# First units of a gated cross-attention block in another order on all engines: ScalarE widens the first quantised inputs, the query halves are projected first, and group 1's weights are prepared after the first unit's heads

## The chip, the cores and the metric

One core of a Trainium2 chip (trn2) runs one program. Its engines are TensorE (PE in the profile, PEld its weight loads), VectorE (DVE), ScalarE (ACT), GpSimd (POOL) and SyncE (SP), which only issues DMAs here. Each runs its own list of instructions in the written order and waits on semaphores for the others. The metric is the device time in microseconds (us) of one execution, the median of several. For the kernel before that is 700.87 us (three runs, 699.86 to 701.37).

## What is computed

The part that matters is the attention on 4 batches of 256 rows of 256 values; a mixture of 8 experts (2 per row) follows it.

```python
ln_out = _ln(hidden_states, ln_w, ln_b)
q = _fp8_linear_pertensor(ln_out, wq, wq_scale, q_in_scale)      # per head: _ln(q, qln_w, qln_b); the same for k
v = _fp8_linear_pertensor(ln_out, wv, wv_scale, v_in_scale)
core = _gqa(q, k, v)                                             # softmax(q k / sqrt(d)) v, 16 query heads on 8 groups
qx = _ln(_fp8_linear_pertensor(ln_out, wqx, wqx_scale, qx_in_scale), qxln_w, qxln_b)
kx, vx = split(einsum(cond, w_kv_x)); kx = _ln(kx, kxln_w, kxln_b)
xout = _gqa(qx, kx, vx)
catq = _div_clamp_fp8(cat(core, xout), proj_smooth)
x = x + tanh(g_xattn[0]) * einsum(catq, wproj) * (proj_in_scale * proj_w_scale)
x = x + tanh(g_ffn[0]) * moe(_layernorm(x))
```

`_fp8_linear_pertensor` divides its input by a scale per column, clips it to 448, rounds it to bf16 and then to fp8, and multiplies by the weights.

## The kernel before, in words

**Units.** The attention is cut into 32 units: unit u = 4g + b is head group g (of 8) on batch b (of 4). A unit has two row tiles of 128 rows (st = 0, 1). For each unit TensorE projects queries (`project_q`, L335) and keys and values (`project_kv`, L347 and, for the other input, L351), turns the heads (`turn_heads`, L408), multiplies scores (`scores`, L379), turns probabilities (`turn_probs`, L394) and multiplies values (L419). ScalarE sums the squares of the heads (`square_q` L671, `square_kv` L679, with the copy of the values L684), GpSimd takes the inverse root (`power`, L1425 and L1427), VectorE multiplies by it (`normalise_q` L947, `normalise_kv` L956 to L963), ScalarE scales the turned heads (`affine`, L714), and GpSimd and VectorE split them into a high and a low part (`heads_hi` L1444 and `split_heads` L981, L985). Scores then go through `row_max` (L990, VectorE), `exps` (L698, ScalarE), the inverse of the sum (L995, VectorE) and `scale_probs` (L1433, GpSimd).

**Inputs.** The rows of x come in three chunks: chunks 0 and 1 are two row tiles each (batches 0 and 1), chunk 2 is the other four. A chunk is normalised by rows (VectorE for chunk 0, ScalarE's `row_scale`, L777, for the others; the inverse root is GpSimd's `row_power`, L1484 and L1486, and `row_shift`, L1492 and L1494), turned on TensorE (`turn_input`, L456), scaled by ScalarE (`affine_in`, L754), clipped and rounded by VectorE (`quantise_in`, L1098 and L1104) and widened to fp32r by GpSimd (`widen_in`, L1509) into the tile `xq`, part by part: parts 0 to 3 are chunk 0, parts 4 to 7 chunk 1, 8 to 15 chunk 2. The other input, ctx, is split by ScalarE (`split_ctx`, L761) and VectorE (`ctx_rest`, L1118).

**Weights.** A group's weights are loaded raw into the tile `spare` (in the code `w_raw`), summed (`sum_weights`, L1050, L1053), centred and scaled in blocks of 128 columns (`centre_weights`, L1061, L1063, on VectorE; half of group 0's, `centre_first`, L1502, on GpSimd), and split in four parts into a high part (`weights_hi`, L743, ScalarE) and a low part (`weights_lo`, L1071, VectorE) in `w_ring`. SyncE loads group g's raw weights when the low parts of group g - 1 are done (`w_ready`).

**What sets the order.** Nothing is scheduled by a program: each engine's list is written by hand, for the start line by line and for units 1 to 28 in a loop (`steps`, L238). The change touches only what stands ahead of that loop.

## Time and profile before

| | us |
|---|---|
| median of three runs | 700.87 (699.86 to 701.37) |
| span of the profiled execution | 698.4 |
| what lies around it (median less span) | 2.5 |
| TensorE busy | 640.8 (92%) |
| VectorE busy | 600.3 (86%) |
| ScalarE busy | 550.0 (79%) |
| GpSimd busy | 464.4 (67%) |

The profile is of one execution on the core. "Busy" leaves out waits on semaphores. Times in a timeline are from the start of the span, and a row that stands for several instructions ("x4") gives in its second column the time from the start of the first to the end of the last. In brackets stands how long the engine had been idle before the row and which instruction of which engine ended that. PEclk is TensorE's granted clock as a share of full speed (2.4 GHz).

### The profile page before, as it was taken

How to read it: one execution, taken by the hardware profiler on the slowest of the kernel's cores; microseconds unless marked ns; L12 is line 12 of the kernel's file. 1: busy time of each engine (PE TensorE's matmuls, PEld its weight loads, DVE VectorE, ACT ScalarE, POOL GpSimd, SP SyncE). 2: the span in 40 equal slices, each digit the busy share in tenths (PEclk: the TensorE clock that was granted, in tenths of full speed). 3: DMA queues.
4: the chain of work that ended last, by engine and by line, in shares of the span. 5: the costliest groups of instructions: out<-in, count | busy, mean ns of one | idle time of the engine just before them, and what ended most of it. 6: DMA issues, size and time to landing. Idle time of an engine off the chain costs nothing. (4 is left out here: it accounts for less than half of the span.)

```text
span 698.4 us, 14919 instructions
## 1 busy us (share of the span) xinstructions
PE 640.8 (92%) x4548; PEld 586.4 (84%) x4549; DVE 600.3 (86%) x1387; ACT 550.0 (79%) x1927; POOL 464.4 (67%) x646
## 2 busy tenths in 40 slices
PE   1579999999999999999999999999998569999994
PEld 0578899999999999999999999999977457888883
DVE  7787899999989999998999999888898777777772
ACT  5787889988998999899899989988874145566671
POOL 4777777688677768867776886787664425554542
PEclk9969999999999999999999999999999569999998
DMA  7101101021020101102000110100098402333232
GB/s 224 61 1 52 41 1 31 2 61 32 1 61 2 31 1 62 31 1 61 1 32 1 54 44 1 61 1 1 1 376 317 159 30 47 53 53 52 46 42 26
DMA packets 35509, 37.72 MB, mean 54 GB/s; under 512 B 2704, under 2 KB 30352, under 8 KB 35440
## 3 DMA queue, kind: packets, MB, share of 16 engines
q1 hardware_dynamic: 31024, 30.84, 13.3%
q0 software_dynamic: 4416, 6.03, 5.4%
q8 instruction: 34, 0.56, 0.3%
q14 instruction: 35, 0.29, 0.1%
...
## 5 line engine op out<-in xcount | busy, mean ns | idle before, releaser
L1433 POOL TENSOR_SCALAR shared<-shared,rsum 128x256 f32<-128x256 f32 x256 | 143.5, 572 | 55.6 <-DVE rsum L995 50.6
L698 ACT ACTIVATE shared<-s,nmax 128x256 f32<-128x256 f32 x256 | 122.2, 498 | 23.2 <-DVE nmax L990 23.1
L1427 POOL TENSOR_TENSOR rstd<-rstd,half 128x7 f32<-128x7 f32 (+1 forms) x64 | 87.9, 1374 | 5.3
L990 DVE TENSOR_REDUCE nmax<-s 128x2 f32<-128x512 f32 x128 | 86.5, 678 | 2.8 <-PE s L379 2.6
L1000 DVE TENSOR_TENSOR pt_lo<-t,pt_hi 128x512 fp32r<-128x512 f32 x124 | 84.1, 678 | 1.9 <-ACT pt_hi L706 0.9
L706 ACT CAST pt_hi<-t 128x512 fp32r<-128x512 f32 x124 | 74.0, 597 | 9.8 <-PE t L394 7.3
L714 ACT ACTIVATE shared<-route_bank,head_w 128x512 f32<-128x512 f32 (+1 forms) x124 | 81.5, 689 | 0.0
L394 PE MATMUL t<-ident,shared 128*128 128x128 f32 x496 | 75.8, 276 | 5.8 <-POOL shared L1433 2.5
L985 DVE TENSOR_TENSOR qk_lo<-shared,qk_hi 128x512 fp32r<-128x512 f32 x96 | 78.2, 814 | 2.5 <-POOL qk_hi L1444 1.4
L335 PE MATMUL pj_a<-w_ring,xq 128*128 128x256 f32 x488 | 72.7, 292 | 6.8 <-POOL xq L1509 6.8
L1984 DVE TENSOR_TENSOR w_lo<-expert_w,w_hi 128x1024 fp32r<-128x1024 f32 x46 | 56.3, 1225 | 25.8 <-ACT w_hi L1861 25.1
L379 PE MATMUL s<-qk_hi 128*128 128x256 f32 x256 | 77.9, 304 | 0.2 <-DVE qk_lo L985 0.2
L379 PE MATMUL s<-qk_hi,qk_lo 128*128 128x256 f32 x256 | 72.7, 284 | 0.0
L379 PE MATMUL s<-qk_lo,qk_hi 128*128 128x256 f32 x256 | 72.6, 284 | 0.0
L335 PEld LDWEIGHTS pj_a<-w_ring,xq 128*128 128x128 f32 x488 | 63.5, 193 | 7.3 <-POOL xq L1509 7.2
L438 PE MATMUL acc_bank<-wp_ring,cq 128*128 128x256 f32 x496 | 69.4, 283 | 0.0
L394 PEld LDWEIGHTS t<-ident,shared 128*128 128x128 f32 x496 | 57.7, 141 | 13.7 <-issue 3.7
L729 ACT ACTIVATE y_bf<-o_bank,inv_smooth 128x256 bf16<-128x256 f32 x128 | 54.2, 482 | 18.5 <-PE o_bank L419 18.0
L1451 POOL TENSOR_SCALAR cq<-y_bf 128x512 fp32r<-128x512 f16 x64 | 39.7, 620 | 42.2 <-DVE y_bf L1010 42.1
L438 PEld LDWEIGHTS acc_bank<-wp_ring,cq 128*128 128x128 f32 x496 | 65.4, 190 | 2.5
L671 ACT ACTIVATE start<-pj_a 128x128 bf16<-128x128 f32 x244 | 64.6, 290 | 2.9 <-PE pj_a L335 2.9
L947 DVE TENSOR_TENSOR start<-pj_a,rstd 128x512 f32<-128x512 f32 x61 | 41.9, 687 | 21.6 <-POOL rstd L1427 21.1
...
## 6 DMA issues: line engine op xcount, KB each, us to landing
...
```

Source lines behind the costliest of these rows:

```text
L335: m = pe.matmul(to[:, c0:c0 + 2 * D], xq[:, typ, k, t0:t0 + P], w_ring[:, par, part, k, c0:c0 + 2 * D], start=i == 0, stop=i == 3)
L379: m = pe.matmul(s_bank[st][:, h * S:(h + 1) * S], l[:, qc:qc + P], r[:, kc:kc + S], start=i == 0, stop=i == 2)
L394: m = pe.transpose(to[:, c:c + P], probs[:, st, h * S + kt * P:h * S + (kt + 1) * P], ident[:])
L438: m = pe.matmul(to, cq[:, b % 2, a, h * S + st * P:h * S + (st + 1) * P], wp_ring[:, par, part, 2 * a + h, :], start=n == 0, stop=n == 7)
L698: e = act.activation(probs[:, st, h * S:(h + 1) * S], s_bank[st][:, h * S:(h + 1) * S], ACT.Exp, bias=nmax[:, st, h:h + 1], accum_out=psum ...
L706: act.copy(pt_hi[:, :, st * P:(st + 1) * P], turned(u, a, st)[:].rearrange("p (n s) -> p n s", n=4)).then_inc(pthi_done, 1)
L714: m = act.activation(qk[:, at + c0:at + c0 + n], src[:, c0:c0 + n], ACT.Identity, scale=head_w[:, 2 * w:2 * w + 1], bias=head_w[:, 2 * w + ...
L985: dve.tensor_tensor(qk_lo[:, to], qk[:, c], qk_hi[:, to].bitcast(F32), ALU.subtract).then_inc((qsplit_done, ksplit_done, xsplit_done)[i], 1)
L990: dve.tensor_reduce(nmax[:, st, :], s_bank[st][:].rearrange("p (h t) -> p h t", h=2), AX, ALU.max, negate=True).then_inc(max_done, 1)
L1000: dve.tensor_tensor(pt_lo[:, :, c], turned(u, a, st)[:].rearrange("p (n s) -> p n s", n=4), pt_hi[:, :, c].bitcast(F32), ALU.subtract).the ...
L1427: pool.tensor_tensor(rstd[:, st, c], rstd[:, st, c], half[:, c], ALU.pow).then_inc(rstd_ready, 1)
L1433: m = pool.tensor_scalar(probs[:, st, c], probs[:, st, c], rsum[:, st, h:h + 1], 1.0, ALU.mult, ALU.mult)
```

## The change

Four things change in the written lists ahead of unit 1. ScalarE widens parts 0 to 3 (`widen_first`), and GpSimd keeps parts 4 to 15; chunk 1's rows are normalised by GpSimd and no longer by ScalarE. TensorE projects the queries of both row tiles of the first unit ahead of its keys and values, and group 0's weight parts are made in the order 2, 0, 3, 1 (`FIRST_PARTS`). Further on, unit 0's first `power`, `normalise_q` and `normalise_kv` come earlier in the lists of GpSimd and VectorE. Group 1's raw weights are summed and centred by VectorE, and split by ScalarE, behind the first unit's heads. Semaphores follow: `own_q_centred`, `first_q_ready` and `first_widened` are new. SyncE's list of DMAs is the same.

```diff
--- before.py
+++ after.py
...
+        FIRST_PARTS = (2, 0, 3, 1)
...
@@ -459,19 +462,22 @@
             pe.wait_ge(cols_loaded, 32)
             turn_input(0)
             turn_input(1)
-            pe.wait_ge(xq_ready, 4)
-            pe.wait_ge(w_ready, 1)
+            pe.wait_ge(first_widened, 2)
+            pe.wait_ge(first_q_ready, 1)
             for n in range(2):
                 project_q(0, 0, 0, n, early_banks[n][0], 0)
-                if n == 0:
-                    pe.wait_ge(ctx_split, 1)
+            pe.wait_ge(first_widened, 3)
+            pe.wait_ge(w_ready, 1)
+            pe.wait_ge(ctx_split, 1)
+            for n in range(2):
                 project_kv(0, 0, 0, n, early_banks[n][1], 0)
-            pe.wait_ge(xq_ready, 8)
+            pe.wait_ge(xq_ready, 2)
+            project_q(1, 0, 1, 0, o_bank, 0)
+            pe.wait_ge(xq_ready, 4)
             pe.wait_ge(ctx_split, 2)
-            project_q(1, 0, 1, 0, o_bank, 0)
             project_kv(1, 0, 1, 0, acc_bank, 0)
+            turn_heads(0, 0, 0, s_bank[0])
             turn_input(2)
-            turn_heads(0, 0, 0, s_bank[0])
             turn_heads(0, 0, 1, s_bank[1])
             turn_heads(0, 0, 2, pj_b)
             project_q(1, 0, 1, 1, pj_a, 1)
...
@@ -750,7 +757,7 @@
                 c, col_i, src, to = input_tile(n)
                 act.wait_ge(zt_done, c + 1)
                 if n >= 20:
-                    act.wait_ge(xq_ready, n - 11)
+                    act.wait_ge(xq_ready, n - 15)
                 act.activation(to, src, ACT.Identity, scale=in_scale[:, col_i:col_i + 1],
                                bias=in_shift[:, col_i:col_i + 1]).then_inc(xq_y, 1)
 
@@ -770,9 +777,15 @@
                 square_q(v, st, early_banks[n][0])
                 square_kv(v, v, st, early_banks[n][1])
 
+            def widen_first(m):
+
+                _, _, y, to = input_part(m)
+                act.wait_ge(xq_grid, m + 1)
+                act.activation(to, y.rearrange("p (k t) -> p k t", k=to.shape[1]), ACT.Copy, scale=1.0 / GRID).then_inc(first_widened, 1)
+
             def row_scale(c):
 
-                act.wait_ge(ln_shift, c)
+                act.wait_ge(ln_shift, 1)
                 for t in range(*chunks[c]):
                     m = act.activation(acc[:, t, :], acc[:, t, :], ACT.Identity, scale=lnr[:, t:t + 1], bias=ln_mr[:, t:t + 1])
                 m.then_inc(z_ready, 1)
@@ -780,24 +793,33 @@
             act.wait_ge(consts_ready, 1)
             for n in range(8):
                 affine_in(n)
-            row_scale(1)
             weights_hi(0, 0, 2)
+            weights_hi(0, 0, 0)
+            for n in range(8, 10):
+                affine_in(n)
+            widen_first(0)
+            widen_first(1)
             weights_hi(0, 0, 3)
-            weights_hi(0, 0, 0)
+            for n in range(10, 12):
+                affine_in(n)
             weights_hi(0, 0, 1)
             split_ctx(0)
-            for n in range(8, 16):
+            widen_first(2)
+            square_q(0, 0, early_banks[0][0])
+            for n in range(12, 14):
                 affine_in(n)
+            square_q(0, 1, early_banks[1][0], other_junk[0])
+            square_kv(0, 0, 0, early_banks[0][1])
+            for n in range(14, 16):
+                affine_in(n)
+            square_kv(0, 0, 1, early_banks[1][1], other_junk[1])
+            widen_first(3)
             split_ctx(1)
-            square(0)
+            row_scale(2)
             act.wait_ge(v0_scaled, 1)
             act.copy(v0_w[:, 0], v0_raw).then_inc(v0_high, 1)
-            square(1)
-            row_scale(2)
+            square(2)
             split_ctx(2)
-            square(2)
-            weights_hi(1, 1, 0)
-            weights_hi(1, 1, 1)
             affine(0, 0, s_bank[0])
             act.wait_ge(v0_ready, 1)
             affine(0, 1, s_bank[1])
@@ -806,6 +828,8 @@
             for n in range(16, 20):
                 affine_in(n)
 
+            weights_hi(1, 1, 0)
+            weights_hi(1, 1, 1)
             weights_hi(1, 1, 2)
             weights_hi(1, 1, 3)
             exps(0, 0, 0)
...
@@ -1063,15 +1087,19 @@
                         m = dve.tensor_scalar(w, w, w_scale[:, k, at:at + 1], None, ALU.mult)
                 if n == later_blocks(g)[-1]:
                     m.then_inc(w_centred, 1)
+                elif g == 0 and n == 3:
+                    m.then_inc(own_q_centred, 1)
 
             def weights_lo(g, par, c):
-                dve.wait_ge(w_hi_done, 4 * g + ((c + 2) % 4 if g == 0 else c) + 1)
+                dve.wait_ge(w_hi_done, 4 * g + (FIRST_PARTS.index(c) if g == 0 else c) + 1)
                 k, c0 = c // 2, (c % 2) * BLK // 2
                 c1 = min(c0 + BLK // 2, width(g))
                 m = dve.tensor_tensor(w_ring[:, par, 1, k, c0:c1], w_raw[:, k, c0:c1],
                                       w_ring[:, par, 0, k, c0:c1].bitcast(F32), ALU.subtract)
                 if c == (1 if g == 0 else 3):
                     m.then_inc(w_ready, 1)
+                elif g == 0 and c == 0:
+                    m.then_inc(first_q_ready, 1)
 
             def row_stats(c):
 
@@ -1148,33 +1176,35 @@
             sum_weights(0, 1)
             sum_weights(0, 0)
             dve.wait_ge(w_scales_ready, 1)
-            centre_weights(0, 0, (0, 1, 2, 3) + later_blocks(0))
-            quantise_in(0, 4)
+            centre_weights(0, 0, (0, 1, 2, 3))
+            quantise_in(0, 2)
             weights_lo(0, 0, 2)
+            weights_lo(0, 0, 0)
+            centre_weights(0, 0, later_blocks(0))
+            quantise_in(2, 4)
             weights_lo(0, 0, 3)
-            weights_lo(0, 0, 0)
             weights_lo(0, 0, 1)
             ctx_rest(0)
+            quantise_in(4, 6)
             row_stats(2)
-            quantise_in(4, 8)
-            ctx_rest(1)
             dve.wait_ge(v0_loaded, 16)
             dve.tensor_tensor(v0_raw, v0_raw, w_scale[:, :, 7:8].broadcast_to([P, KT, D]), ALU.mult).then_inc(v0_scaled, 1)
+            normalise_q(0, 0, 0, early_banks[0][0])
+            normalise_kv(0, 0, 0, early_banks[0][1])
+            quantise_in(6, 8)
+            ctx_rest(1)
+            normalise_q(0, 0, 1, early_banks[1][0])
+            normalise_kv(0, 0, 1, early_banks[1][1])
             dve.wait_ge(v0_high, 1)
             dve.tensor_tensor(v0_w[:, 1], v0_raw, v0_w[:, 0].bitcast(F32), ALU.subtract).then_inc(v0_ready, 1)
+            ctx_rest(2)
+            split_heads(0, 0, 0)
+            split_heads(0, 0, 1)
             for k in range(KT):
                 sum_weights(1, k)
             centre_weights(1, 0, (0, 1, 2, 3) + later_blocks(1))
-            normalise_q(0, 0, 0, early_banks[0][0])
-            normalise_kv(0, 0, 0, early_banks[0][1])
-            centre_weights(1, 1, (0, 1, 2, 3))
-            normalise_q(0, 0, 1, early_banks[1][0])
-            normalise_kv(0, 0, 1, early_banks[1][1])
-            ctx_rest(2)
-            split_heads(0, 0, 0)
-            split_heads(0, 0, 1)
-            centre_weights(1, 1, later_blocks(1))
             split_heads(0, 0, 2)
+            centre_weights(1, 1, (0, 1, 2, 3) + later_blocks(1))
             quantise_in(8, 10)
 
             row_max(0, 0, 0)
...
@@ -1485,12 +1515,19 @@
                 pool.wait_ge(var_eps0, c + 1)
                 pool.tensor_tensor(lnr[:, t], lnr[:, t], half[:, t], ALU.pow).then_inc(ln_rstd, 1)
 
+            def row_normalise(c):
+
+                pool.wait_ge(ln_rstd, c + 1)
+                for t in range(*chunks[c]):
+                    m = pool.tensor_scalar(acc[:, t, :], acc[:, t, :], mv[:, t, 0:1], lnr[:, t:t + 1], ALU.subtract, ALU.mult)
+                m.then_inc(z_ready, 1)
+
             def row_shift(c):
 
                 t = slice(*chunks[c])
                 pool.wait_ge(ln_rstd, c + 1)
                 pool.tensor_tensor(ln_mr[:, t], mv[:, t, 0], lnr[:, t], ALU.mult).then_inc(ln_shift_part, 1)
-                pool.wait_ge(ln_shift_part, c)
+                pool.wait_ge(ln_shift_part, 1)
                 pool.tensor_scalar(ln_mr[:, t], ln_mr[:, t], -1.0, 1.0, ALU.mult, ALU.mult).then_inc(ln_shift, 1)
 
             def centre_first():
@@ -1500,7 +1537,8 @@
                 for n in range(CENTRED[0]):
                     w, at = w_raw[:, 1, n * D:(n + 1) * D], SCALES[0][n]
                     m = pool.tensor_scalar(w, w, w_mean[:, 1, n:n + 1], w_scale[:, 1, at:at + 1], ALU.add, ALU.mult)
-                m.then_inc(first_centred, 1)
+                    if n in (3, CENTRED[0] - 1):
+                        m.then_inc(first_centred, 1)
 
             def widen_in(m):
 
@@ -1512,21 +1550,20 @@
             pool.wait_ge(ones_set, 1)
             row_power(0)
             row_power(1)
-            row_shift(1)
+            row_normalise(1)
             centre_first()
-            for m in range(4):
+            for m in range(4, 6):
                 widen_in(m)
             row_power(2)
             row_shift(2)
-            for m in range(4, 8):
+            power(0, 0)
+            for m in range(6, 8):
                 widen_in(m)
-            power(0, 0)
-            pool.wait_ge(normkv_done, 1)
             power(0, 1)
             wp_hi(0, 0, 0)
             wp_hi(0, 0, 1)
             heads_hi(0, 0, 0)
-            pool.wait_ge(normkv_done, 2)
+            pool.wait_ge(normkv_done, 1)
             power(1, 0)
             heads_hi(0, 0, 2)
             for m in range(8, 12):
@@ -1536,7 +1573,7 @@
             for m in range(12, 16):
                 widen_in(m)
             scale_probs(0, 0, 1)
-            pool.wait_ge(normkv_done, 3)
+            pool.wait_ge(normkv_done, 2)
             power(1, 1)
             scale_probs(0, 1, 0)
             wp_lo(0, 0, 0)
```

TensorE, start of the program, before: after the input is turned, the eight query matmuls of row tile 0 (into `pj_a`), its keys and values (`pj_b`), then row tile 1 (`s_0`).

```order
L335 MATMUL pj_a<-w_ring,xq 128x256 x8
L347 MATMUL pj_b<-w_ring,xq 128x256 x4
L351 MATMUL pj_b<-w_ring,ctx_hi 128x256 x2
L351 MATMUL pj_b<-w_ring,ctx_lo 128x256
L351 MATMUL pj_b<-w_ring,ctx_hi 128x256 x2
L351 MATMUL pj_b<-w_ring,ctx_lo 128x256
L335 MATMUL s_0<-w_ring,xq 128x256 x8
```

After:

```order
L338 MATMUL pj_a<-w_ring,xq 128x256 x8
L338 MATMUL s_0<-w_ring,xq 128x256 x8
L350 MATMUL pj_b<-w_ring,xq 128x256 x4
L354 MATMUL pj_b<-w_ring,ctx_hi 128x256 x2
L354 MATMUL pj_b<-w_ring,ctx_lo 128x256
L354 MATMUL pj_b<-w_ring,ctx_hi 128x256 x2
L354 MATMUL pj_b<-w_ring,ctx_lo 128x256
L350 MATMUL s_1<-w_ring,xq 128x256 x4
```

The eight query matmuls of row tile 1 now stand ahead of row tile 0's keys and values.

VectorE, from the low part of v0's weights (`cq`) to the second unit tile's normalise, before (`w_sum`, `w_mean` and `spare` with L1050 to L1063 are group 1's weights, `start<-pj_a,rstd` is the first normalise and `start<-s_0,rstd` the second):

```order
L1164 TENSOR_TENSOR cq<-shared,cq 128x256
L1050 TENSOR_REDUCE w_sum<-spare 128x5
L1053 TENSOR_SCALAR w_mean<-w_sum 128x5
L1050 TENSOR_REDUCE w_sum<-spare 128x5
L1053 TENSOR_SCALAR w_mean<-w_sum 128x5
L1061 TENSOR_SCALAR spare<-spare,w_mean,w_scale 128x128 x5
L1063 TENSOR_SCALAR spare<-spare,w_scale 128x128 x2
L947 TENSOR_TENSOR start<-pj_a,rstd 128x512
L956 TENSOR_SCALAR k_next<-pj_b,rstd 128x128
L957 TENSOR_TENSOR start<-pj_b,rstd 128x256
L963 TENSOR_TENSOR v_lo<-pj_b,v_hi 128x128
L1061 TENSOR_SCALAR spare<-spare,w_mean,w_scale 128x128 x4
```

After, from the scaling of v0's weights (`shared`) on (`start<-start` with L1126 and L1132 is the quantising of parts 6 and 7, `ctx_lo` the low part of ctx chunk 1):

```order
L1191 TENSOR_TENSOR shared<-shared,w_scale 128x256
L971 TENSOR_TENSOR start<-pj_a,rstd 128x512
L980 TENSOR_SCALAR k_next<-pj_b,rstd 128x128
L981 TENSOR_TENSOR start<-pj_b,rstd 128x256
L987 TENSOR_TENSOR v_lo<-pj_b,v_hi 128x128
L1126 TENSOR_SCALAR start<-start 128x512 x2
L1132 TENSOR_SCALAR start<-start 128x512 x2
L1146 TENSOR_TENSOR ctx_lo<-shared,ctx_hi 128x2x256
L971 TENSOR_TENSOR start<-s_0,rstd 128x512
```

Group 1's sums and first blocks no longer stand between v0's weights and the first normalise; quantising of parts 6 and 7 and a low part of ctx now stand between the first and the second normalise.

VectorE, the heads of unit 0 up to the quantising ahead of the first row max, before:

```order
L985 TENSOR_TENSOR qk_lo<-shared,qk_hi 128x512
L981 CAST qk_hi<-shared 128x512
L985 TENSOR_TENSOR qk_lo<-shared,qk_hi 128x512
L1061 TENSOR_SCALAR spare<-spare,w_mean,w_scale 128x128
L1063 TENSOR_SCALAR spare<-spare,w_scale 128x128 x2
L985 TENSOR_TENSOR qk_lo<-shared,qk_hi 128x512
```

After:

```order
L1009 TENSOR_TENSOR qk_lo<-shared,qk_hi 128x512
L1005 CAST qk_hi<-shared 128x512
L1009 TENSOR_TENSOR qk_lo<-shared,qk_hi 128x512
L1074 TENSOR_REDUCE w_sum<-spare 128x5
L1077 TENSOR_SCALAR w_mean<-w_sum 128x5
L1074 TENSOR_REDUCE w_sum<-spare 128x5
L1077 TENSOR_SCALAR w_mean<-w_sum 128x5
L1085 TENSOR_SCALAR spare<-spare,w_mean,w_scale 128x128 x5
L1087 TENSOR_SCALAR spare<-spare,w_scale 128x128 x2
L1009 TENSOR_TENSOR qk_lo<-shared,qk_hi 128x512
L1085 TENSOR_SCALAR spare<-spare,w_mean,w_scale 128x128 x5
L1087 TENSOR_SCALAR spare<-spare,w_scale 128x128 x2
```

The sums of group 1 and its ten centred blocks with their four plain scalings now stand between the second and the third `qk_lo` and behind the third, where one block and two plain scalings stood.

## Rows read from the trace of the kernel before

**Rows 1.** The page: the span, and from its part 5 GpSimd's scaling of probabilities

```profile
span 698.4 us, 14919 instructions
...
L1433 POOL TENSOR_SCALAR shared<-shared,rsum 128x256 f32<-128x256 f32 x256 | 143.5, 572 | 55.6 <-DVE rsum L995 50.6
```

**Rows 2.** Windows: length, busy us of each engine, PEclk, DMA share, GB/s

```profile
0.00:41.70 41.70, 18.41 (x114) 16.78 (x115) 31.39 (x115) 29.45 (x91) 24.63 (x40) 0.96 0.38 119
41.70:66.00 24.30, 19.00 (x123) 17.71 (x121) 19.37 (x48) 18.73 (x77) 18.85 (x25) 0.79 0.00 1
66.00:540.00 474.00, 467.91 (x3535) 439.68 (x3535) 439.94 (x1011) 420.54 (x1637) 351.10 (x524) 1.00 0.15 50
```

**Rows 3.** Waits from 66 to 540 us: the only one that a DMA ended

```profile
DVE w_sum L1050 <- DMA spare<-in_wT: 0.2, 1, 0.2
```

**Rows 4.** Waits from 30 to 66 us: in total, times, longest

```profile
DVE start L947 <- POOL rstd L1427: 5.7, 3, 3.8
```

**Rows 5.** Timeline of TensorE: start, us, line, tiles, forms, count, idle before

```profile
21.31 2.08 PE L335 MATMUL pj_a<-w_ring,xq 128*128 128x256 f32 x8 [6.83 <-POOL xq L1509]
23.18 1.05 PE L347 MATMUL pj_b<-w_ring,xq 128*128 128x256 f32 x4
```

**Rows 6.** Timeline of ScalarE, the start of the program

```profile
8.58 3.75 ACT L754 ACTIVATE start<-t,in_shift,in_scale 128x256 bf16<-128x256 f32 x8 [2.98 <-PE t L456]
...
13.69 2.18 ACT L743 CAST w_ring<-spare 128x512 fp32r<-128x512 f32 x4 [0.39 <-POOL spare L1502]
...
27.39 0.33 ACT L679 ACTIVATE start<-s 128x128 bf16<-128x128 f32 x1
...
28.28 2.15 ACT L777 ACTIVATE acc<-acc,ln_mr,lnr 128x256 f32<-128x256 f32 x4
30.26 1.11 ACT L761 CAST ctx_hi<-shared 128x1024 fp32r<-128x1024 f32 x1
...
35.54 0.78 ACT L714 ACTIVATE shared<-s,head_w 128x512 f32<-128x512 f32 x1 [1.17 <-PE s L408]
```

**Rows 7.** Timeline of GpSimd, the start of the program

```profile
10.59 3.07 POOL L1502 TENSOR_SCALAR spare<-spare,w_mean,w_scale 128x128 f32<-128x128 f32 x7 [0.78 <-DVE w_mean L1053]
14.94 6.31 POOL L1509 TENSOR_SCALAR xq<-start 128x512 fp32r<-128x512 f16 x4 [1.28 <-DVE start L1104]
...
23.57 2.36 POOL L1509 TENSOR_SCALAR xq<-start 128x512 fp32r<-128x512 f16 x4
...
26.58 1.73 POOL L1427 TENSOR_TENSOR rstd<-rstd,half 128x7 f32<-128x7 f32 x1
```

**Rows 8.** Timeline of VectorE, up to the first projections

```profile
11.79 2.46 DVE L1061 TENSOR_SCALAR spare<-spare,w_mean,w_scale 128x128 f32<-128x128 f32 x7
...
15.79 2.48 DVE L1071 TENSOR_TENSOR w_ring<-spare,w_ring 128x512 fp32r<-128x512 f32 x4
...
18.80 1.39 DVE L1081 BATCH_NORM_STATS2 stat<-acc 128x6 f32<-128x256 f32 x4
```

**Rows 9.** Timeline of VectorE, from v0's low part to the first row max

```profile
26.54 0.42 DVE L1164 TENSOR_TENSOR cq<-shared,cq 128x256 fp32r<-128x256 f32 x1 [3.00 <-ACT cq L794]
26.88 0.81 DVE L1050 TENSOR_REDUCE w_sum<-spare 128x5 f32<-128x640 f32 x1
...
28.74 1.36 DVE L1061 TENSOR_SCALAR spare<-spare,w_mean,w_scale 128x128 f32<-128x128 f32 x5
...
30.41 0.68 DVE L947 TENSOR_TENSOR start<-pj_a,rstd 128x512 f32<-128x512 f32 x1
...
31.80 1.10 DVE L1061 TENSOR_SCALAR spare<-spare,w_mean,w_scale 128x128 f32<-128x128 f32 x4
33.80 0.69 DVE L947 TENSOR_TENSOR start<-s,rstd 128x512 f32<-128x512 f32 x1 [0.90 <-POOL rstd L1427]
...
37.05 0.69 DVE L985 TENSOR_TENSOR qk_lo<-shared,qk_hi 128x512 fp32r<-128x512 f32 x1 [0.65 <-POOL qk_hi L1444]
...
38.12 0.69 DVE L985 TENSOR_TENSOR qk_lo<-shared,qk_hi 128x512 fp32r<-128x512 f32 x1
...
41.66 1.28 DVE L990 TENSOR_REDUCE nmax<-s 128x2 f32<-128x512 f32 x2
```

23 lines of the change are left out of this document (13 added, 10 removed).

## The prediction, made before the changed kernel ran

> **What bounds the kernel now.** I first read the windows [rows 2]. From 66 to 540 us TensorE is busy for 467.9 of 474.0 us at the full clock, and only one wait there was ended by a DMA, for 0.2 us [rows 3]. So that stretch neither absorbs nor adds anything: whatever the start of the program gains or loses is passed on. Up to 66 us it is different. TensorE is busy for 18.4 of the first 41.7 us and for 19.0 of the next 24.3, VectorE for 31.4 and 19.4. The end of that start is therefore set by a chain across the engines, which is read from the timelines.
>
> The reader is to see two things in them. At the front, TensorE stands idle for 6.83 us before its first projection at 21.31, released by GpSimd's widening [rows 5]; four widenings took 6.31 us there against 2.36 us for the next four, while VectorE worked through its low parts without a break [rows 7, 8]. That is the stall that the change goes at. Behind it, VectorE waits for 3.00 us before 26.54, then does group 1's sums and centring, and only then the first normalise at 30.41, although GpSimd's inverse root is done at 28.3 (26.58 + 1.73) [rows 7, 9]. After another 0.90 us of waiting the second normalise comes at 33.80, the second `qk_lo` at 38.12, and the first row max at 41.66 [rows 9]. I take the first row max as the milestone: from it on, VectorE and GpSimd pass the unit to each other.
>
> **Step A, the first projection.** VectorE now centres only four blocks first: 11.79 + 4 x 0.35 (2.46 / 7) = 13.2. Four parts were quantised between 14.2 and 15.8, so two cost 0.8: 14.0. Two low parts at 0.62 (2.48 / 4): 15.2 [rows 8]. On ScalarE the first high part waits for GpSimd's fourth block, 10.59 + 4 x 0.44 = 12.4 [rows 7]; two high parts at 0.54 and two input scalings at 0.47 give 14.4 [rows 6]. No row of before shows a widening on ScalarE. It writes 512 columns, so it lies between the cast of 512 columns (0.54) and the scaling of 512 columns (0.78) [rows 6]; I take 0.54 since it reads no table of scales: 15.5. With 0.5 for handovers the first projection starts at 16.0 in place of 21.31, 5.3 earlier. The higher price makes it 16.5, which nothing below depends on. Normalising chunk 1's rows on GpSimd is not shown either: between nothing beyond the two small operations that it replaces and 1.8 us (four blocks at 0.44 for two rows of 256 columns), which at worst moves GpSimd's centring by half a us; the same slack covers it.
>
> **Step B, the first and the second normalise.** TensorE needs 1.87 us for eight query matmuls (21.31 to 23.18) [rows 5], so 3.7 for both halves, about 2.2 for ten key and value matmuls, and ScalarE 0.9 for the squares (27.39 to 28.28) [rows 6]: the squares of row tile 0 are there at about 22.9. But GpSimd's list has the row statistics of chunk 2 ahead of `power(0, 0)`, and these wait for VectorE: from 15.2, three blocks 1.05, quantising 0.8, two low parts 1.2, a low part of ctx 0.6 (18.2 to 18.8 in before), quantising 0.8, and the row statistics 1.4 and an aggregation of about 0.3 give 21.4 [rows 8]. GpSimd's four small operations took 2.3 us (from 21.25, the end of its first widenings, to 23.57), so 23.7, and `power` 2.0 (the 1.73 and the small one ahead of it): 25.7 [rows 7]. First normalise at 25.8 in place of 30.41, 4.6 earlier. It takes 1.4 (30.41 to 31.80) [rows 9], then quantising 0.8 and ctx 0.6 follow: 28.6. GpSimd's widenings of parts 6 and 7 now stand behind `power(0, 0)`. They are ready at 28.0, and by the stretch of 6.31 us I hold them until VectorE pauses at 28.6; 2 x 0.59 gives 29.8, and `power(0, 1)` 1.9 more [rows 7]. Second normalise at 31.8 in place of 33.80: the lead has shrunk to 2.0.
>
> The Trainium skill has a rule on this, in the page "SBUF — State Buffer", section "SBUF: two separate sides": the port pair that VectorE and GpSimd share is an exclusive lock, and whoever starts first has it for one whole instruction. By that rule a widening would wait for one VectorE instruction, some 0.6 us, and the second normalise would come at most 0.6 earlier than I have it; the first widenings of this trace lost 4 us in one go [rows 7], so the trace agrees with a lock but not with a handover after each instruction. The sum goes by the row.
>
> **Step C, the heads.** TensorE's keys and values of unit 1 wait for that widening, 29.8. TensorE has little to do from about 24 on, so I price its ten matmuls at the half-speed pace of [rows 5], 2.2 us; at full speed they would be 1.1 less. ScalarE: squares 0.9 and the high part of ctx 1.0, so the first scaled heads start at 34.0 in place of 35.54 [rows 6]. The low part of ctx (1024 columns, twice 0.6) keeps VectorE until 35.2, and GpSimd's high part of the heads (about 0.6) follows: the first `qk_lo` at 35.9 in place of 37.05. From there to the end of the second `qk_lo` before took 1.7 us [rows 9], so 37.6 in place of 38.7. The lead is 1.1.
>
> **Step D, what is put in.** Here VectorE now does group 1's sums (26.88 to 28.74, 1.86), five blocks and two plain scalings (28.74 to 30.41, 1.67), the third `qk_lo` 0.6, and the same 1.67 once more: 5.8 us, and then the quantising, 0.8 [rows 9]. First row max at 37.6 + 5.8 + 0.8 = 44.2 in place of 41.66, **2.5 later**. Before, this work lay in the waits of 3.00 and 0.90 us and ahead of the first normalise; those waits are now longer and empty, and the work lies on the path. It costs 5.2 us in all (1.86 + 2 x 1.67), of which before only one block and two plain scalings, 0.8, stood behind the second `qk_lo`. ScalarE's high parts of group 1, moved behind the scaled inputs, stand ahead of `exps`, but are done while ScalarE would wait for the row max.
>
> **Step E, on to 66 us.** VectorE's waits for GpSimd's inverse root sum to 5.7 us there, the longest 3.8 [rows 4], and VectorE is idle for 4.9 us of 24.3 [rows 2]. Since GpSimd in turn waits for VectorE's row sums, as it does all along (55.6 us in the whole span, 50.6 of them so ended) [rows 1], a late VectorE delays the release of its own waits. I take 0.3 as given back, with 0 and 1.5 as the ends. The sum is 2.5 - 0.3 = +2.2 on a span of 698.4: 700.6. The median of the runs before, 700.87, stands 2.5 above that span, and I carry that: **703.1 us**.
>
> **The rivals.**
> *The front lead holds.* If the second normalise keeps the whole lead of 4.6 (29.2), the second `qk_lo` ends at 34.1, and the row max comes at 40.7, 1.0 earlier than before. With TensorE less often at half speed between 41.7 and 66 (granted 0.79 there [rows 2]) another 0.8 may go: 698.4 - 1.8 + 2.5 = 699.1. For it: the stall of 6.83 is the largest wait of the start. Against: GpSimd's widenings 6 and 7 and `power` alone take 3.1 us behind the first normalise's quantising. It decides where the second normalise comes before about 29.5 (31.8 less the 2.5 of step D), since the row max would then come as before.
> *The delay is absorbed.* If VectorE's waits give back 1.6 of their 5.7 us, +0.9: 701.8. For it, the 4.9 us idle; against it, the circular wait of step E.
> *It is worse.* GpSimd's widenings run beside VectorE's centring and quantising at the pace of the first four (1.6 each in place of 0.6), two ahead of the second normalise and two ahead of the first probabilities: + 2 to + 3, 705.6. It decides where VectorE has no pause between 26 and 29. This and the sum above lie on the slower side.
> *The order does nothing*, because ScalarE, with the added widenings, starts the first projection no earlier and the group 1 work falls into other waits: 700.9.
>
> **How the numbers follow.** Chances: the sum 0.56, lead holds 0.13, absorbed 0.14, worse 0.14, nothing 0.03. The sum's own range is 701.8 (full clock in step C, 1.0 given back) to 704.5 (nothing given back, ScalarE's widening at 0.78, a unit's `power` held by VectorE). The range that leaves out two in ten is 700.0 to 705.8: the upper half of "worse" and most of "lead holds" lie outside. A measurement of this kernel can tell about 0.2%, 1.4 us, from no change. Faster than 699.5 is two thirds of "lead holds": 0.09. Within 0.2% (699.5 to 702.3) are the rest of it, most of "absorbed", "nothing", and the lower edge of the sum: 0.19. Slower: 0.72.
>
> **What the profile of the changed kernel would show.** Step A: the first query matmul between 15.5 and 17. Step B: the first normalise at about 26 with GpSimd's inverse root as the releaser, the second at about 32. Step C: the second `qk_lo` ends at 37 to 38. Step D: VectorE's sums of group 1 directly behind it, and the first row max at 44. Step E: from there on each unit about 2 us later than before. I am wrong if the second normalise comes before 30, if VectorE has a gap of over 2 us in the stretch where I put the group 1 work, or if the row max at 44 is no longer seen as a delay at 66 us.

## The result: 2.9 to 3.5 us slower

The changed kernel took 703.99 us (median of six runs, 702.77 to 705.65) against 700.46 for the kernel before (six runs, 699.37 to 701.70): a ratio of 1.0050, 95% interval 1.0036 to 1.0065. Timed again beside the experiments it took 702.70 against 699.80: 1.0039 (1.0024 to 1.0054). The forecast was 703.1, within 700.0 to 705.8, and slower with a chance of 0.72.

**The profile after.** First the windows, cut at the same events as [rows 2] (first row max, 24.4 us behind it, then 474 us): length, busy time of TensorE, its weight loads, VectorE, ScalarE and GpSimd, PEclk, DMA share, GB/s.

```profile
0.00:44.80 44.80, 20.15 (x128) 18.55 (x129) 31.69 (x114) 30.26 (x93) 21.64 (x35) 0.92 0.36 111
44.80:69.20 24.40, 17.80 (x107) 16.94 (x108) 17.78 (x48) 19.02 (x77) 18.44 (x23) 0.72 0.01 1
69.20:543.20 474.00, 467.95 (x3534) 439.50 (x3534) 440.14 (x1011) 421.16 (x1636) 353.27 (x526) 1.00 0.15 50
```

The long stretch is what it was: 467.95 us of TensorE in 474. The start is longer by about 3 us, and in the window behind it VectorE and GpSimd have less work in the same time, not more.

TensorE's and VectorE's timelines, with the places that answer to [rows 5] and [rows 9] (start, duration of the row, idle before it and what ended that):

```profile
16.12 1.23 PE L338 MATMUL pj_a<-w_ring,xq 128*128 128x256 f32 x4 [3.78 <-ACT xq L784]
```

```profile
25.84 0.69 DVE L971 TENSOR_TENSOR start<-pj_a,rstd 128x512 f32<-128x512 f32 x1 [3.66 <-POOL rstd L1457]
...
31.70 0.69 DVE L971 TENSOR_TENSOR start<-s,rstd 128x512 f32<-128x512 f32 x1 [2.97 <-POOL rstd L1457]
...
36.15 0.69 DVE L1009 TENSOR_TENSOR qk_lo<-shared,qk_hi 128x512 fp32r<-128x512 f32 x1 [0.52 <-POOL qk_hi L1474]
...
37.22 0.69 DVE L1009 TENSOR_TENSOR qk_lo<-shared,qk_hi 128x512 fp32r<-128x512 f32 x1
37.83 0.82 DVE L1074 TENSOR_REDUCE w_sum<-spare 128x5 f32<-128x640 f32 x1
38.68 0.58 DVE L1077 TENSOR_SCALAR w_mean<-w_sum 128x5 f32<-128x5 f32 x1
...
44.84 1.28 DVE L1014 TENSOR_REDUCE nmax<-s 128x2 f32<-128x512 f32 x2
```

The first projection is 5.2 us earlier, the first normalise 4.6, the second 2.1, the first `qk_lo` 0.9. Then group 1's sums start, directly behind the second `qk_lo`, and the first row max is 3.2 us late. VectorE stands idle for 3.66 and 2.97 us ahead of the two normalises: the work that used to lie there now lies at 37.83. GpSimd's timeline shows who sets those two waits:

```profile
20.03 1.21 POOL L1547 TENSOR_SCALAR xq<-start 128x512 fp32r<-128x512 f16 x2 [4.90 <-DVE start L1132]
...
22.32 1.04 POOL L1516 TENSOR_TENSOR lnr<-lnr,half 128x4 f32<-128x4 f32 x1
...
24.32 1.49 POOL L1457 TENSOR_TENSOR rstd<-rstd,half 128x7 f32<-128x7 f32 x1
28.01 1.78 POOL L1547 TENSOR_SCALAR xq<-start 128x512 fp32r<-128x512 f16 x2 [2.21 <-DVE start L1132]
...
30.16 1.50 POOL L1457 TENSOR_TENSOR rstd<-rstd,half 128x7 f32<-128x7 f32 x1
...
38.61 0.62 POOL L1474 TENSOR_SCALAR qk_hi<-shared 128x512 fp32r<-128x512 f32 x1
```

Behind the row statistics (22.32) comes the first `power` (24.32), which releases the first normalise. Then GpSimd waits 2.21 us until VectorE has quantised parts 6 and 7, widens them, and does the second `power` (30.16), which releases the second.

One small row is worth reading. VectorE's mean at 38.68 takes 0.58 us where the same operation elsewhere takes 0.17; it ends at 39.26, and GpSimd's high part of the heads runs from 38.61 to 39.23. I read it so that this instruction on 5 columns was held until GpSimd's had finished. The page "SBUF — State Buffer" of the Trainium skill, section "SBUF: two separate sides", describes such a lock, held for a whole instruction; here the trace agrees.

### The profile page after: what moved, and what is told of

Same layout as the page of the kernel before. It is cut to its first block and busy times, and to the rows that moved or that the text cites. A ratio compares the mean times of both kernels' runs of the same rounds, so it can differ in the third digit from the quotient of the medians.

```text
span 703.8 us, 14916 instructions
## 1 busy us (share of the span) xinstructions
PE 640.9 (91%) x4548; PEld 585.4 (83%) x4549; DVE 599.2 (85%) x1387; ACT 551.7 (78%) x1929; POOL 474.0 (67%) x642
## 5 line engine op out<-in xcount | busy, mean ns | idle before, releaser
L2132 POOL DMA_INDIRECT out<-y_sb,slot_out x23 | 49.8, 2165 | 43.1 <-DMA out<-y_sb,slot_out 41.6
```

## The experiments

All stand beside runs of the kernel before on the same chip. "Row max" is the start of unit 0's first row max on VectorE, "load" the moment near 168 us at which SyncE loads a group's weights into `wp_raw`, "store" the moment at which it stores the normalised rows for the expert stage, which follows the attention; all three are from one profile each.

| kernel | row max, us | load, us | store, us | time, us | ratio to before (95%) |
|---|---|---|---|---|---|
| before | 41.66 | 167.81 | 546.82 | 699.8 to 700.5 | 1 |
| changed | 44.84 | 170.81 | 549.48 | 703.99 | 1.0050 (1.0036 to 1.0065) |
| changed, again | 45.79 | 171.43 | 549.70 | 702.70 | 1.0039 (1.0024 to 1.0054) |
| only_g1 | 43.61 | 169.32 | 547.62 | 701.21 | 1.0032 (1.0015 to 1.0048) |
| g1_back | 42.71 | 169.39 | 548.07 | 701.17 | 1.0016 (1.0003 to 1.0029) |
| sums_twice | 46.37 | 172.27 | 550.51 | 703.77 | 1.0060 (1.0039 to 1.0081) |
| quantise_early | 43.42 | 169.26 | 548.58 | 701.51 | 1.0022 (1.0010 to 1.0034) |
| pool_widens | 45.95 | 171.99 | 552.35 | 704.43 | 1.0061 (1.0046 to 1.0077) |
| early_parts | 41.54 | 167.31 | 545.65 | 699.09 | 0.9990 (0.9977 to 1.0002) |
| late_g1 | 38.68 | 166.45 | 546.19 | 698.80 | 0.9983 (0.9972 to 0.9993) |
| late_g1_sum | 38.50 | 165.89 | 544.42 | 698.37 | 0.9975 (0.9964 to 0.9986) |
| late_all | 37.44 | 166.18 | 545.59 | 698.33 | 0.9967 (0.9956 to 0.9977) |

**only_g1: the move of group 1's work alone.** VectorE, on the kernel before (ScalarE's `weights_hi(1, 1, 0)` and `(1, 1, 1)` move as in the change):

```diff
-            for k in range(KT):
-                sum_weights(1, k)
-            centre_weights(1, 0, (0, 1, 2, 3) + later_blocks(1))
             normalise_q(0, 0, 0, early_banks[0][0])
...
             split_heads(0, 0, 1)
-            centre_weights(1, 1, later_blocks(1))
+            for k in range(KT):
+                sum_weights(1, k)
+            centre_weights(1, 0, (0, 1, 2, 3) + later_blocks(1))
             split_heads(0, 0, 2)
+            centre_weights(1, 1, (0, 1, 2, 3) + later_blocks(1))
```

> The kernel before with only the move of group 1's work (VectorE's sums and centring behind the second qk_lo and the third, ScalarE's two high parts behind the scaled inputs), nothing else of the change. Theory: the first normalise is no longer behind the sums and comes at 28.4 in place of 30.4 (GpSimd's inverse root), the second qk_lo ends at 36.6, then 5.8 + 0.8 us follow and 0.4 for the means: row max at 43.6, 1.9 later than before, and the time about 702.3. Rival (the cost of the change sits in its new front order, not in this move): no more than 0.5 us from the kernel before.

```profile
28.41 0.69 DVE L947 TENSOR_TENSOR start<-pj_a,rstd 128x512 f32<-128x512 f32 x1 [1.38 <-POOL rstd L1426]
...
31.78 0.69 DVE L947 TENSOR_TENSOR start<-s,rstd 128x512 f32<-128x512 f32 x1 [1.90 <-POOL rstd L1426]
...
35.99 0.69 DVE L985 TENSOR_TENSOR qk_lo<-shared,qk_hi 128x512 fp32r<-128x512 f32 x1
...
43.61 0.68 DVE L990 TENSOR_REDUCE nmax<-s 128x2 f32<-128x512 f32 x1
```

The two normalises are 2 us earlier than in [rows 9], each now released by GpSimd, the second `qk_lo` ends at 36.6, and the row max comes at 43.61: the theory's numbers to the tenth. The median, 701.21, is 1.1 us under the 702.3 that was expected. The move alone costs 2.0 us at the row max, 1.5 us at the load and 1.5 to 4.8 in a thousand of the time. Of the loss of the change that is about half: 3.2 and 4.1 us at the row max and 3.0 and 3.6 us at the load, in its two profiles.

**g1_back: the changed kernel with that work back in the waits.**

```diff
+            for k in range(KT):
+                sum_weights(1, k)
             normalise_q(0, 0, 0, early_banks[0][0])
             normalise_kv(0, 0, 0, early_banks[0][1])
             quantise_in(6, 8)
             ctx_rest(1)
+            centre_weights(1, 0, (0, 1, 2, 3) + later_blocks(1))
+            centre_weights(1, 1, (0, 1, 2, 3))
             normalise_q(0, 0, 1, early_banks[1][0])
...
             split_heads(0, 0, 1)
-            for k in range(KT):
-                sum_weights(1, k)
-            centre_weights(1, 0, (0, 1, 2, 3) + later_blocks(1))
+            centre_weights(1, 1, later_blocks(1))
             split_heads(0, 0, 2)
-            centre_weights(1, 1, (0, 1, 2, 3) + later_blocks(1))
```

> The changed kernel with only VectorE's group 1 work put back into waits ahead of the second normalise: both sums ahead of the first normalise (where the changed kernel waits 3.66 us), ten centred or scaled blocks ahead of the second (where it waits 2.97 us), and only the last three behind the second qk_lo, as in the kernel before. Theory (the inserted work is what costs): the second qk_lo stays near 38, the first row max falls from 44.8 to about 41, and the time from 704.0 to 700.3 or less, between 0.5 and 1 us under the kernel before. Rival (the lead of the front is lost between the first and the second normalise in any case, or VectorE's work there holds GpSimd's widening): the second normalise slips by 1.5 us or more and the time stays above 702.

```profile
25.26 0.82 DVE L1074 TENSOR_REDUCE w_sum<-spare 128x5 f32<-128x640 f32 x1 [2.15 <-DMA spare<-in_wT]
...
29.91 2.01 DVE L1085 TENSOR_SCALAR spare<-spare,w_mean,w_scale 128x128 f32<-128x128 f32 x5
...
...
33.72 0.68 DVE L971 TENSOR_TENSOR start<-s,rstd 128x512 f32<-128x512 f32 x1
...
42.71 0.68 DVE L1014 TENSOR_REDUCE nmax<-s 128x2 f32<-128x512 f32 x1
```

It gains 2.1 us at the row max on the first profile of the changed kernel (3.1 on the second) and takes about two thirds of the loss in time away, but it does not pass the kernel before, and the row max is 1.7 us behind the 41 that was expected. Both halves of the wait were smaller than they looked: the sums wait 2.15 us for group 1's DMA, and the blocks take 0.40 us each (2.01 for five) beside GpSimd's work in place of 0.27, so that the second normalise slips to 33.72, where it was in the kernel before. Of that slip of 2.0 us, 0.9 is this execution's later start (its first `power` begins at 25.24, against 24.32). The rival was right on the slip and wrong on the time, which it put above 702. The two experiments add up, as near as single profiles can tell: 2.0 for the move and 1.05 for the new order at the front without it make 3.0 us at the row max, against 3.2 and 4.1; at the load 1.5 and 1.6 make 3.1, against 3.0 and 3.6.

**quantise_early: who loses the lead of the front.**

```diff
+            quantise_in(6, 8)
             normalise_q(0, 0, 0, early_banks[0][0])
             normalise_kv(0, 0, 0, early_banks[0][1])
-            quantise_in(6, 8)
             ctx_rest(1)
```

> The changed kernel with one edit: parts 6 and 7 quantised ahead of the first normalise, in VectorE's wait of 3.66 us. Theory (the lead of the front is lost because these two parts stand behind the first normalise, and GpSimd's power(0, 1) behind their widening): second normalise 1.8 us earlier than in the changed kernel, first row max 1 to 2 us earlier, near 43, and the time 1 to 2 us under the changed kernel, near 701.5. Rival (GpSimd is as late for other reasons, or ScalarE's ctx part is next): under 0.5 us gained.

```profile
26.90 0.69 DVE L971 TENSOR_TENSOR start<-pj_a,rstd 128x512 f32<-128x512 f32 x1 [1.18 <-POOL rstd L1457]
...
30.36 0.69 DVE L971 TENSOR_TENSOR start<-s,rstd 128x512 f32<-128x512 f32 x1 [1.39 <-POOL rstd L1457]
...
43.42 0.68 DVE L1014 TENSOR_REDUCE nmax<-s 128x2 f32<-128x512 f32 x1
```

The second normalise comes at 30.36 against 31.70 and 32.65 in the two profiles of the changed kernel, the row max at 43.42 against 44.84 and 45.79, and the ratio is 1.0022 against 1.0050 and 1.0039. The start of this execution is as late as in the second profile (first normalise at 26.90 and 26.81). From the first to the second normalise it is 3.46 us, against 5.86 and 5.84 in the two profiles: 2.4 us of the front's lead is what this one line had cost. In the time it gains 2.0 us on the first runs, clear of their interval, and 1.2 us on the second, in intervals that overlap.

**sums_twice: is the place really on the path?** Two more sums over the same weights, into a tile that nobody reads, ahead of the others:

```diff
+            dve.wait_ge(w_loaded, loaded_w(1))
+            for k in range(KT):
+                dve.tensor_reduce(sum_again[:, k, 0:CENTRED[1]], ...)
             for k in range(KT):
                 sum_weights(1, k)
```

> The changed kernel with two more sums over group 1's raw weights on VectorE at the same place, 1.7 us of work whose result nobody reads. Theory (this place is on the path to the end and nothing absorbs it): row max 1.7 later, time 1.5 to 1.8 us above the changed kernel, 705.6. Rival (the next waits give it back): under 0.5 us.

```profile
38.30 1.54 DVE L1206 TENSOR_REDUCE sum_again<-spare 128x5 f32<-128x640 f32 x2
...
46.37 1.28 DVE L1015 TENSOR_REDUCE nmax<-s 128x2 f32<-128x512 f32 x2
```

From the end of the second `qk_lo` to the row max it is 8.07 us, against 6.61 in the second profile of the changed kernel (39.18 to 45.79): 1.5 more for 1.5 put in. The start of this execution is earlier than in that profile, so its row max is only 0.6 us behind it (46.37 against 45.79); at the load it is 0.8 (172.27 against 171.43), and at the store 0.8 (550.51 against 549.70): nothing was given back. The median, 703.77, is not the 705.6 that was expected, and 1.0060 overlaps with 1.0039 and 1.0050: the place is shown by the trace, not by the times.

**pool_widens: is ScalarE's widening what frees the front?**

```diff
-            widen_first(0)
-            widen_first(1)
...
+            for m in range(4):
+                _, _, y, to = input_part(m)
+                pool.wait_ge(xq_grid, m + 1)
+                pool.tensor_scalar(to, y.rearrange(...), 1.0 / GRID, 1.0, ALU.mult, ALU.mult).then_inc(first_widened, 1)
             for m in range(4, 6):
                 widen_in(m)
```

> The changed kernel with parts 0 to 3 widened by GpSimd again (behind its centring, ahead of parts 4 and 5), all else as changed. Theory (step A: VectorE's unbroken run holds GpSimd's widening, and the first projection needs it): the first projection comes at about 21 in place of 16.1, the first normalise near 30, the second near 35.5, the first row max near 48.5, and the time 3 to 4.5 us above the changed kernel. Rival (GpSimd's row statistics for chunk 2 bound the first normalise, and it need not wait for projections): first projection late, first row max within 1 us of 44.8 and the time within 1 us.

```profile
16.95 1.44 PE L338 MATMUL pj_a<-w_ring,xq 128*128 128x256 f32 x5 [4.59 <-POOL xq L1554]
```

```profile
15.69 1.20 POOL L1554 TENSOR_SCALAR xq<-start 128x512 fp32r<-128x512 f16 x2
17.52 1.63 POOL L1554 TENSOR_SCALAR xq<-start 128x512 fp32r<-128x512 f16 x2 [0.63 <-DVE start L1128]
```

```profile
17.56 2.13 DVE L1093 TENSOR_TENSOR w_ring<-spare,w_ring 128x512 fp32r<-128x512 f32 x2
...
26.78 0.69 DVE L967 TENSOR_TENSOR start<-pj_a,rstd 128x512 f32<-128x512 f32 x1 [3.65 <-POOL rstd L1453]
...
32.62 0.69 DVE L967 TENSOR_TENSOR start<-s,rstd 128x512 f32<-128x512 f32 x1 [2.96 <-POOL rstd L1453]
```

The theory fell. GpSimd widens the four parts in 1.20 and 1.63 us, the first projection starts at 16.95 (16.12 and 17.10 with ScalarE's widening), and both normalises and the row max are within 0.2 us of the second profile of the changed kernel. Two things are left that free the first projection. It asks for two parts and two low parts in place of four and four: the fourth part is there at 19.15 and the fourth low part at 19.7, 2.7 us later than the start here. And the 4 us stall of [rows 7] does not come back, which would make up the rest of the 4.4 us from 21.31 to 16.95. No run tries either by itself. VectorE's two low parts at 17.56 take 2.13 us here in place of about 1.3: the two engines hold each other here for one instruction at a time. Why it was so long in the kernel before, where a widening stood beside four low parts in a row, stays open.

Its time is still 1.7 us above that of the changed kernel timed beside it (1.0061 against 1.0039, in intervals that overlap), and neither the row max nor the load, 0.6 us later, explains that. The windows of the last stretch ahead of the store point to it (columns as above): the kernel before, with three of its microseconds by themselves, the changed kernel again, and this one.

```profile
536.00:548.00 12.00, 10.20 (x71) 9.16 (x69) 9.19 (x47) 3.51 (x9) 3.47 (x8) 0.81 0.29 106
540.00:543.00 3.00, 3.00 (x14) 3.00 (x15) 1.92 (x14) 0.18 (x1) 0.00 (x0) 0.50 0.00 0
```

```profile
536.00:548.00 12.00, 10.16 (x73) 8.76 (x71) 9.37 (x34) 3.74 (x10) 3.41 (x7) 1.00 0.58 215
```

```profile
524.00:536.00 12.00, 9.98 (x65) 8.70 (x65) 11.56 (x28) 7.48 (x24) 6.92 (x14) 0.94 1.06 399
536.00:548.00 12.00, 11.16 (x67) 10.31 (x66) 7.76 (x29) 4.21 (x10) 3.04 (x6) 0.78 0.51 193
```

The granted clock there is 0.81, 1.00 and 0.78 of full speed, so part of the stretch ran at 1.2 GHz in the first and the third and none in the second. The third stores its rows 2.65 us later than the second, though the two are 0.5 apart when SyncE begins to load the experts (509.4 and 508.9). What the start gives or takes is blurred by some 2 us here. The kernel before has such a stretch, too (0.50 from 540 to 543 us), ahead of its own store at 546.82, so the distances at the store may be too small for the slower kernels; the load near 168 us lies ahead of all this and is the better measure. That the clock is the cause was not tried by itself.

**changed_again: the same kernel, no edit.**

> The changed kernel itself once more, for a second profile and times beside those of the other kernels of this call. What is open: its first profile is 5.4 us longer than that of before, but stands only 2.7 us behind it when the normalised rows are stored (549.5 against 546.8). If the expert stage really costs more in the changed kernel, this profile shows the same 2.7 us between that point and the end; if that was one execution, the stretch behind it is within 1 us of the 151.6 us of before.

VectorE in the second profile (first and second normalise, the end of the second `qk_lo`, row max):

```profile
26.81 0.69 DVE L971 TENSOR_TENSOR start<-pj_a,rstd 128x512 f32<-128x512 f32 x1 [3.65 <-POOL rstd L1457]
...
32.65 0.69 DVE L971 TENSOR_TENSOR start<-s,rstd 128x512 f32<-128x512 f32 x1 [2.96 <-POOL rstd L1457]
...
39.18 0.81 DVE L1074 TENSOR_REDUCE w_sum<-spare 128x5 f32<-128x640 f32 x1
...
45.79 1.27 DVE L1014 TENSOR_REDUCE nmax<-s 128x2 f32<-128x512 f32 x2
```

SyncE's store of the normalised rows, in the first and in the second profile of the changed kernel:

```profile
549.48 0.37 SPq L316 DMA_DIRECT2D x_hat<-acc  x1
```

```profile
549.70 0.37 SPq L316 DMA_DIRECT2D x_hat<-acc  x1
```

Behind it the first profile has another 154.3 us (703.8 less 549.5), the second 151.2 (700.9 less 549.7), the kernel before 151.6. The expert stage need not cost more: the first profile was of the longest of six executions (705.65), and the second does not show the extra 2.7 us.

**Four steps to a version that is faster than both.** early_parts is quantise_early with group 1's sums ahead of the second normalise, its centring as in the change (five blocks and two scalings on either side of the third `qk_lo`), and ScalarE's high part of ctx chunk 2 ahead of unit 1's squares:

```diff
             ctx_rest(1)
+            for k in range(KT):
+                sum_weights(1, k)
             normalise_q(0, 0, 1, early_banks[1][0])
...
             split_heads(0, 0, 1)
-            for k in range(KT):
-                sum_weights(1, k)
             centre_weights(1, 0, (0, 1, 2, 3) + later_blocks(1))
```

> A version meant to keep the lead of the front: the changed kernel with parts 6 and 7 quantised ahead of the first normalise (in VectorE's wait of 3.66 us), so that GpSimd can widen them as soon as its power is done; group 1's sums ahead of the second normalise, its centring still behind the second and the third qk_lo; ScalarE's ctx chunk 2 ahead of the squares of unit 1. Theory: GpSimd widens at 25.8 and is done with power(0, 1) at 28.8, the second normalise comes at 29.8 behind the sums, the second qk_lo ends near 34.5, the row max comes near 39.3, 2.4 earlier than in the kernel before, and the time is 698 to 699. Rival (the chain behind the row max is bound elsewhere, by ScalarE's scaled inputs or the slow TensorE): row max early, time not under 700.

```profile
30.45 0.68 DVE L971 TENSOR_TENSOR start<-s,rstd 128x512 f32<-128x512 f32 x1
...
35.41 0.43 DVE L1005 CAST qk_hi<-shared 128x512 fp32r<-128x512 f32 x1 [0.83 <-ACT shared L721]
...
36.49 1.66 DVE L1085 TENSOR_SCALAR spare<-spare,w_mean,w_scale 128x128 f32<-128x128 f32 x5
...
41.54 0.68 DVE L1014 TENSOR_REDUCE nmax<-s 128x2 f32<-128x512 f32 x1
```

The row max came 2.2 us later than expected, 0.1 us ahead of the kernel before. The second `qk_lo` had to wait, since TensorE turns the input of chunk 2 ahead of the second row tile's heads (ScalarE's release at 35.41), and the ten blocks are still on the path. The store of the rows is 1.2 us earlier than before; in the time the interval includes no difference.

late_g1 takes the centring, too, out of the way, and turns the heads first. VectorE's list against early_parts (TensorE turns the second row tile's heads ahead of the input of chunk 2, and ScalarE's four high parts move behind unit 0's exponentials):

```diff
             split_heads(0, 0, 1)
-            centre_weights(1, 0, (0, 1, 2, 3) + later_blocks(1))
             split_heads(0, 0, 2)
-            centre_weights(1, 1, (0, 1, 2, 3) + later_blocks(1))
...
             row_sum(0, 0, 1)
-            weights_lo(1, 1, 0)
-            weights_lo(1, 1, 1)
...
+            centre_weights(1, 0, (0, 1, 2, 3) + later_blocks(1))
             dve.wait_ge(xq_ready, 12)
             normalise_q(1, 1, 1)
...
             row_sum(0, 1, 1)
-            weights_lo(1, 1, 2)
-            weights_lo(1, 1, 3)
+            centre_weights(1, 1, (0, 1, 2, 3) + later_blocks(1))
+            weights_lo(1, 1, 0)
+            weights_lo(1, 1, 1)
             normalise_q(2, 2, 0, o_bank)
...
             rest_v0(1, s_bank[1])
+            weights_lo(1, 1, 2)
+            weights_lo(1, 1, 3)
```

> early_parts with group 1's centring no longer ahead of the first row max at all: five blocks and two scalings ahead of unit 1's second normalise, as many behind unit 0's last row sums, with ScalarE's high parts and VectorE's low parts behind them; TensorE turns the second row tile's heads ahead of the input of chunk 2. Theory (VectorE's list is the path up to the row max, and its waits of 1.5 and 3.9 us between 53 and 61 us can take the work): first row max near 38 in place of 41.5, unit 2's first normalise near 58 in place of 60.5, time 1.5 to 3 us under early_parts, 696 to 697.5. Rival (the chain behind the row max is bound by something else that does not move, or the moved work fills not waits but path): less than 0.7 us gained.

The row max is where it was expected, 38.68, and unit 2's first normalise is at 57.23 (60.31 before), but the time gained only 0.5 us on early_parts by the ratios, in overlapping intervals: the rival.

late_g1_sum adds one move:

```diff
             centre_weights(1, 0, (0, 1, 2, 3) + later_blocks(1))
+            row_sum(0, 1, 0)
             dve.wait_ge(xq_ready, 12)
             normalise_q(1, 1, 1)
             normalise_kv(1, 1, 1)
             probs_lo(0, 0, 1)
-            row_sum(0, 1, 0)
             row_sum(0, 1, 1)
```

> late_g1, and the inverse of unit 0's third row sum on VectorE ahead of unit 1's second normalise in place of behind it, so that GpSimd's scaling of probabilities, which waits 2.35 us for it in every version so far, can start at once. Theory (VectorE and GpSimd wait for each other there): unit 2's first normalise another 1.5 to 2.3 us earlier, time 1 to 2 us under late_g1. Rival (TensorE at half speed, or ScalarE, sets the pace there by now): under 0.5 us.

```profile
50.85 0.94 POOL L1463 TENSOR_SCALAR shared<-shared,rsum 128x256 f32<-128x256 f32 x2 [1.91 <-DVE rsum L1019]
...
54.30 2.79 POOL L1457 TENSOR_TENSOR rstd<-rstd,half 128x7 f32<-128x7 f32 x1
```

The wait was longer in late_g1 than the expectation says, 3.89 us, and the scaling stood at 53.07; it now starts 2.2 us earlier. GpSimd still waits 1.91 us for the row sum, since five blocks stand ahead of it, and the rest of the gain is lost behind: its `power` took 2.79 us in place of 1.52 beside VectorE's two low parts of group 1 (54.47, 1.27 us), so that it ended at 57.09 against 57.19, and unit 2's first normalise did not move (57.13). The 0.4 us in time cannot be told from none.

late_all moves the sums and one step of GpSimd:

```diff
-            for k in range(KT):
-                sum_weights(1, k)
             normalise_q(0, 0, 1, early_banks[1][0])
...
             row_sum(0, 0, 1)
+            for k in range(KT):
+                sum_weights(1, k)
             probs_lo(0, 0, 0)
...
             heads_hi(0, 0, 0)
+            heads_hi(0, 0, 2)
             pool.wait_ge(normkv_done, 1)
             power(1, 0)
-            heads_hi(0, 0, 2)
```

> late_g1_sum with group 1's sums, too, out of the way of unit 0 (in VectorE's wait of 2 us for the first turned probabilities in place of ahead of the second normalise), and GpSimd's high part of the third heads ahead of unit 1's power. Theory (VectorE's and GpSimd's lists are the path up to the first row max): second normalise 0.5 us earlier, third qk_lo 1.3 us earlier, first row max near 36.7 in place of 38.5, and the time 0.5 to 1.5 us under late_g1_sum, 697 to 698. Rival (from the row max on TensorE or the loop's own chain takes over, as half of what late_g1 won was gone by 105 us): under 0.3 us gained.

```profile
60.43 1.28 DVE L1097 TENSOR_TENSOR w_ring<-spare,w_ring 128x512 fp32r<-128x512 f32 x2
```

late_all has the earliest row max (37.44, 4.2 us earlier than before) and a ratio of 0.9967, the best, though not to be told from late_g1_sum's. Of its 4.2 us, 3.5 are left at unit 2's first normalise (56.77 against 60.31) and 2.3 at unit 2's second (62.96 against 65.28). Between the two VectorE has no gap, and the row above shows what lies there: the last two low parts of group 1, which late_g1 moved to this place, 1.2 us. Group 1's work is on the path again, one place further on.

Behind that the three late versions differ. Two windows of late_all, then of late_g1_sum:

```profile
64.00:68.00 4.00, 4.00 (x24) 4.00 (x23) 3.97 (x11) 2.85 (x12) 2.67 (x5) 0.57 0.85 262
66.00:110.00 44.00, 43.81 (x323) 41.01 (x322) 39.61 (x90) 38.44 (x154) 33.76 (x50) 0.98 0.12 36
```

```profile
64.00:68.00 4.00, 3.87 (x30) 3.46 (x30) 3.96 (x11) 3.37 (x17) 2.67 (x5) 1.00 0.80 238
66.00:110.00 44.00, 43.25 (x323) 40.37 (x323) 40.29 (x92) 39.01 (x155) 34.61 (x51) 1.00 0.13 38
```

In late_all TensorE's granted clock is 0.57 from 64 to 68 us (0.58 in late_g1), so most of that stretch ran at 1.2 GHz; in late_g1_sum and in the kernel before it is 1.00. From unit 2's second normalise to SyncE's load near 105 us late_all loses 0.8 us on the kernel before (42.26 against 41.45 us), late_g1_sum 0.1 (41.52). At the load near 168 us the leads are 1.6 (late_all), 1.4 (late_g1) and 1.9 us (late_g1_sum). That the clock takes the 0.8 us was not tried by itself.

Over all kernels a late start is passed on nearly in full: the seven profiles whose row max is 1.05 to 4.7 us late stand 1.45 to 4.5 us late at the load. Of an early start of 3.0 to 4.2 us only 1.4 to 1.9 are left there.

## Why the prediction was right, and where it was not

**Right in the sign and the place.** The path at the start was VectorE's and GpSimd's, not TensorE's; group 1's work had lain in waits and was put on the path. only_g1 and g1_back show that by taking the move out and in, and sums_twice shows the place.

- *Step A*, first projection at 16.0: 16.12 and 17.10. The number held, in part by luck. I had taken the stall of [rows 7] for GpSimd's, cured by ScalarE; pool_widens shows that GpSimd alone does as well. Normalising chunk 1 on GpSimd took 2.44 us, not at most 1.8, and its seven centring blocks behind that 3.97 and 4.94 us in place of 3.07. The first high part so came at 12.98 and 13.95 in place of 12.4; in the first profile the handovers of 0.5 us, which were not there, made up for it.
- *Step B*, normalises at 25.8 and 31.8: 25.84 and 31.70 (26.81 and 32.65 in the second profile). GpSimd's row statistics and then parts 6 and 7 set them; quantise_early confirms the second. I had held the widening until VectorE pauses, by the stretch of [rows 7]; it took 1.78 us in place of 1.21 beside one VectorE instruction, which both the row and a lock for one instruction would give, so this place does not decide between them.
- *Step C*, end of the second `qk_lo` at 37.6: 37.83 (39.18). The lead of 1.1 us was 0.9 in the first profile; in the second it was gone (0.45 later than before).
- *Step D*, 6.6 us from there to the row max: 7.0 in the first profile, of which 0.4 is the held mean, and 6.6 in the second. only_g1 confirms it in the kernel before.
- *Step E*, 0.3 given back by 66 us: nothing was. Unit 2's first normalise is 3.5 us late (63.84 against 60.31), since VectorE's longest wait there, 3.8 us [rows 4], is again 3.86:

```profile
63.84 0.69 DVE L971 TENSOR_TENSOR start<-o_bank,rstd 128x512 f32<-128x512 f32 x1 [3.86 <-POOL rstd L1457]
```

The mis-sized terms are this one and the delay at the row max: 3.2 us in the first profile and 4.1 in the second, in place of 2.5. Of the first, 0.4 is the held mean and 0.2 step C; in the second step D is right to the tenth, and the whole excess is the front's lead, which was put at 1.1 and was not there. At the load near 168 us 3.0 and 3.6 us are left, against a forecast of 2.2, and the time says 1.7 to 4.6 (the two intervals of the ratio). "The lead holds" is ruled out by the second normalise, "it is worse" by the two widenings ahead of it, 1.78 us together and not 3.2, and "the delay is absorbed" by the wait that did not shrink. The time alone excludes "absorbed" (+0.9 us) and "holds", and "worse" (+4.2 to +5.2) only in part.

Two things are in no step, and only the width of the range covered them: that one execution's start can be 1 us later than another's, and the clock in the last stretch of the attention, which goes with 1 to 2 us in a single execution.
